# A fused transformer kernel with another written order of all its calls, and the cross attention's keys loaded from ScalarE's DMA queue

## The reference

```python
# block 0: 8 heads of 40, keys/values from the context, the last 4 context rows apart
hs      = mha(x @ Wq, enc @ Wk, enc @ Wv)                   # "FIRST"
ca_hs1  = mha(ca_q1, x, x)                                  # "CA": queries from the 4 rows
ca_hs2  = mha(ca_hs1 @ Wq, ca @ Wk_ca, ca @ Wv_ca)
x = (hs + ca_hs2) @ Wout + b_out + x
# block 1: 20 heads of 16
h1 = ln(x); x = attn(h1, h1, q1, k1, v1, o1) + x            # "SELF"
h2 = ln(x); x = attn(h2, context, q2, k2, v2, o2) + x       # "CROSS"
h3 = ln(x); a, g = split(h3 @ ff_w1 + ff_b1)
x = (a * gelu(g)) @ ff_w2 + ff_b2 + x                       # FF = 1280
```

## Time and profile before

| | |
|---|---|
| median of 3 runs | 3753.11 us (3748.72 to 3754.11) |
| the profiled execution, its time | 3752.51 us |
| its span, first to last instruction | 3750.7 us |
| mean granted TensorE clock | 0.959 |
| TensorE busy | 3433.0 us, 92% |
| VectorE, ScalarE, GpSimd busy | 61%, 65%, 56% |

### The profile page before, as it was taken

How to read it: one execution, slowest core, us unless ns; L and a number is a source line. 1 busy time by engine, 2 the same in 40 slices (tenths; PEclk the granted TensorE clock), 3 DMA queues, 4 the chain that set the end, 5 groups by cost and what they waited for, 6 DMA issues and landing times.

```text
span 3750.7 us, 114679 instructions
## 1 busy us (share of the span) xinstructions
PE 3433.0 (92%) x38842; PEld 2823.0 (75%) x38842; DVE 2282.8 (61%) x5540; ACT 2431.1 (65%) x4362; POOL 2082.5 (56%) x2307
## 2 busy tenths in 40 slices
PE   7799999999999999999999999999999999999998
PEld 6677777777777777777777777777777777777777
DVE  6566666566666656656665666666566666656664
ACT  3576666667766666776666677666666766666674
POOL 1556555555655555565555556555555655555564
PEclk6899999999999999999999999999999999999999
DMA  5211111221111122211112222111122211112220
GB/s 182 57 42 45 35 44 43 49 53 48 50 34 46 42 49 53 48 51 33 46 41 48 53 49 52 31 47 42 47 53 50 51 31 47 42 46 53 51 50 18
DMA packets 316267, 183.06 MB, mean 49 GB/s; under 512 B 50107, under 2 KB 315379, under 8 KB 315507
## 3 DMA queue, kind: packets, MB, share of 16 engines
q1 hardware_dynamic: 303936, 173.93, 18.4%
q10 hardware_dynamic: 11955, 3.04, 0.4%
HBM read 70.59 MB, written 24.67 MB: 25 GB/s over the span
## 4 chain that ended last, share of the span: by engine, by line
PE 35%; issue 29%; POOL 23%; DVE 8%; DMA 2%; POOLq 1%; ACT 1%; SPq 0%; DVEq 0%; ACTq 0%
PE bank L1487 32%; POOL PT L540 12%; POOL XB L517 2%; DVE mx L1104 2%; POOL cQ L547 2%; POOL cK L547 2%; DMA out<-X 2%; PE bank L1514 1%; POOL XA L517 1%; POOL rstd L598 1%; POOL c L592 1%; DVE OA L1219 1%; DVE hTn L1133 1%; POOL X L517 1%; DVE hTn L1130 1%
## 5 line engine op out<-in xcount | busy, mean ns | idle before, releaser
L540 POOL TENSOR_TENSOR PT<-P,PT 128x512 f16<-128x512 f32 (+1 forms) x924 | 1071.5, 1160 | 603.2 <-ACT PT L811 599.5
L1487 PE MATMUL bank<-hT,w_ff_w 128*128 128x256 f16 x5440 | 637.0, 272 | 0.8 <-DVE hT L1133 0.8
L1104 DVE TENSOR_REDUCE mx<-bank 128x4 f32<-128x512 f32 (+1 forms) x924 | 596.3, 683 | 56.1 <-PE bank L1487 49.4
L1487 PEld LDWEIGHTS bank<-hT,w_ff_w 128*128 128x128 f16 x5440 | 521.4, 98 | 60.7 <-DVE hT L1133 1.2
L1487 PE MATMUL bank<-mxs,pick 84*128 84x128 f16 (+1 forms) x3696 | 553.5, 230 | 0.0
L1487 PE MATMUL bank<-w_ff,F 128*128 128x320 f32 x1360 | 412.2, 438 | 41.6 <-DVE whole L1005 40.4
L1487 PE MATMUL bank<-Qs,Ks 96*128 96x128 f16 x2640 | 404.0, 235 | 15.1 <-DVE mxs L1113 15.1
L1487 PEld LDWEIGHTS bank<-mxs,pick 84*128 84x128 f16 (+1 forms) x3696 | 395.8, 109 | 4.1
L794 ACT ACTIVATE gate<-bank,ff_b,scale 128x256 f32<-128x256 f32 x340 | 187.5, 566 | 304.3 <-PE bank L1487 228.5
L1487 PEld LDWEIGHTS bank<-V,PT 128*128 128x128 f16 (+1 forms) x9504 | 317.0, 96 | 39.5 <-POOL PT L540 13.8
L1487 PE MATMUL bank<-V,PT 128*128 128x17 f16 (+1 forms) x9504 | 341.5, 173 | 0.0
(11 more groups left out here) (289 smaller groups left out, 7386.5 us busy)
## 6 DMA issues: line engine op xcount, KB each, us to landing
Qs<-cQ SPq DMA_DIRECT2D x402, 64.0 KB, 2.6
Ks<-scratch_k SPq DMA_DIRECT2D x99, 160.0 KB, 4.9
Ks<-cK SPq DMA_DIRECT2D x198, 64.0 KB, 2.6
Q0s<-cQ SPq DMA_DIRECT2D x198, 60.0 KB
K0s<-cK SPq DMA_DIRECT2D x198, 60.0 KB
xin<-in_x SPq DMA_DIRECT2D x34, 320.0 KB, 3.6
out<-X SPq DMA_DIRECT2D x64, 160.0 KB, 1.9
xT<-in_xT SPq DMA_DIRECT2D x68, 128.0 KB, 2.1
```

The lines of the kernel that those rows point to most:

```text
L540: nc.gpsimd.tensor_tensor(PT[0:keys, n % PT_SLOTS, 1, :], P[0:keys, n % P_SLOTS, :], PT[0:keys, n % PT_SLOTS, 0, :], ALU.subtract).then_in ...
L1104: nc.vector.tensor_reduce(mx[:, g % 2, 4 * u:4 * u + 4], bank[:, :].rearrange("p (h s) -> p h s", h=4)[:, :, 0:keys], axis=AX.X, op=ALU.ma ...
L1487: return nc.tensor.matmul(o, lhsT, rhs, start=start, stop=stop)
```

## The change

All calls of the loop are put into another order, on every engine, with `BODY` to match; the work of each call is the same. `ff0` is now the first job of a pass and `outM0_1` the last; `K0T1` goes between `outT1_1` and `outM1_0`, `K0T2` and `V0_1` into the cross attention's scores, `mT` and `mB` from behind `Q2T2` into the self attention; `S14` and `S15` stand within the down projection `y1`; `V1_0`, `V1_1` and `T2` go behind `S4`; gelu 2 and 3 go behind the exponentials of `T0` and `T1`. The three loads of the cross attention's keys are issued by ScalarE behind the exponentials of `T13`, no longer by SP.

```diff
 BODY = jobs_of("""
-    Q0T0 XT0_0 XT0_1 S0 Q0T1 Q0T2 K1T0 K1T1 K1T2 Q1T0 Q1T1 Q1T2 S1 ff0 S2 S3 ff1 ff2 mx0 K0T0 ff3 T0
-    V1_0 K0T1 mx1 K0T2 V0_0 T1 V1_1 T2 S4 S5 S6 S7 S8 T3 vca mx2 S9 T4 S10 T5 S11 T6 S12 S13 caT0
-    mx3 T7 T8 T9 T10 T11 T12 T13 caT1 ff4 outT1_0 ff5 ff6 ff7 outT1_1 outM1_0 outM1_1 ff8 XT1_0 ff9
-    XT1_1 s4 Q2T0 Q2T1 Q2T2 mT mB V0_1 K2T0 K2T1 y1 S14 S15 S16 S17 S18 mx4 S19 S20 T14 S21 T15 S22
-    S23 T16 S24 S25 mx5 T17 S26 T18 S27 mx6 T19 T20 T21 T22 p4T T23 T24 mx7 outT2_0 T25 y0 T26
-    outM2_0 V2_0 outT2_1 T27 hs0 outM2_1 outT0_0 hs1 XT2_0 V2_1 outT0_1 outM0_0 K2T2 outM0_1 XT2_1 G
+    ff0 Q0T0 Q0T1 XT0_0 Q0T2 XT0_1 ff1 K1T0 K1T1 S0 S1 K1T2 Q1T0 S2 S3 mx0 Q1T1 Q1T2 V0_0 mx1 T0 T1
+    ff2 ff3 S4 S5 T2 vca S6 S7 V1_0 T3 S8 S9 mx2 S10 K0T0 T4 S11 T5 S12 S13 T6 V1_1 mx3 T7 caT0 caT1
+    T8 mT T9 T10 T11 T12 T13 mB ff4 outT1_0 ff5 ff6 ff7 outT1_1 K0T1 outM1_0 outM1_1 ff8 s4 XT1_0
+    XT1_1 ff9 Q2T0 Q2T1 Q2T2 K0T2 S14 S15 y1 S16 S17 S18 V0_1 K2T0 mx4 S19 S20 S21 T14 S22 S23 K2T1
+    S24 T15 S25 mx5 T16 S26 T17 T18 T19 T20 p4T T21 mx6 S27 T22 T23 y0 mx7 T24 T25 K2T2 outT2_0 V2_0
+    outT2_1 T26 T27 outM2_0 hs0 outM2_1 outT0_0 hs1 V2_1 outM0_0 outT0_1 XT2_0 XT2_1 G outM0_1
 """)
...
             def one_pass(i, stores):
-                load_products(i)
                 put_low(i, "Q0T", 0, Q0s, cQ, Q_PARTS)
...
                 put_split(i, "Q1T", 2, Qs, cQ, Q_PARTS)
+                load_products(i)
                 load_next(i)
                 put_low(i, "K0T", 0, K0s, cK, K_PARTS)
                 put_low(i, "K0T", 1, K0s, cK, K_PARTS)
-                stack_cross_keys(i)
-                put_low(i, "K0T", 2, K0s, cK, K_PARTS)
                 put_split(i, "Q2T", 0, Qs, cQ, Q_PARTS)
                 put_split(i, "Q2T", 1, Qs, cQ, Q_PARTS)
                 put_split(i, "Q2T", 2, Qs, cQ, Q_PARTS)
-                put_out(i, 0, stores)
+                put_low(i, "K0T", 2, K0s, cK, K_PARTS)
...
+            def stack_cross_keys(i):
+                act.wait_ge(k2_put, i * CROSS_STORES + CROSS_STORES)
+                act.wait_ge(j_full, done(i, LOOP_JOBS.number("T13"), "J"))
+                for y, part in enumerate(K_PARTS):
+                    act.dma_start(Ks[y * D1:(y + 1) * D1, :, :],
+                                  s_k2[part, :, :].rearrange("(h e) n -> e h n", e=D1)).then_inc(cross_stacked, 16)
```

More of the change, by code:

```diff
@@ L882, in _ @@
                 links[0] = 0
+                gelu(i, L, 0)
                 high_chunk(i, "Q0T", 0, cQ, CH0[0], FQ0)
+                high_chunk(i, "Q0T", 1, cQ, CH0[1], FQ0)
                 high_blocks(i, "XT0_0", hTn, 0)
+                high_chunk(i, "Q0T", 2, cQ, CH0[2], FQ0)
                 high_blocks(i, "XT0_1", hTn, 1)
-                high_chunk(i, "Q0T", 1, cQ, CH0[1], FQ0)
                 split_context(i)
-                high_chunk(i, "Q0T", 2, cQ, CH0[2], FQ0)
+                gelu(i, L, 1)
                 high_shifted(i, "K1T", 0, cK, 0)
@@ L1397, in _ @@
                 normalise(i, 1)
+                extremes_x(i + 1)
+                extremes_context(i + 1)
+                low_part(i, "V1", 1, V1, HEADS1, D1, V1_FACTOR)
+                low_maxima(i, 3)
                 copy_hT(i, "caT0", 0, CH0)
-                low_maxima(i, 3)
+                copy_hT(i, "caT1", 1, CH0)
+                diagonal(i, L, 2)
                 normalise(i, 2)
-                copy_hT(i, "caT1", 1, CH0)
-                extremes_x(i + 1)
+                step_sizes(i, L)
                 ff(i, L, 4)
@@ L1409, in _ @@
                 low_out(i, 1, 1)
+                low_chunk(i, "K0T", 1, cK, CH0[1], FK0)
                 residual(i, 1, 0)
+                residual(i, 1, 1)
                 norm(i, 1, 0)
-                residual(i, 1, 1)
+                norm(i, 1, 1)
                 ff(i, L, 8)
-                norm(i, 1, 1)
+                scores4(i)
                 low_blocks(i, "XT1_0", hTn, 0)
+                low_blocks(i, "XT1_1", hTn, 1)
                 ff(i, L, 9)
-                low_blocks(i, "XT1_1", hTn, 1)
-                scores4(i)
                 whole_shifted(i, "Q2T", 0, 6)
@@ L1443, in _ @@
                 low_maxima(i, 5)
+                softmax4(i)
                 maxima(i, 26)
+                copy_shares(i)
+                low_maxima(i, 6)
                 maxima(i, 27)
-                low_maxima(i, 6)
-                copy_shares(i)
+                result(i, L, 0)
+                low_maxima(i, 7)
                 normalise(i, 4)
-                low_maxima(i, 7)
+                normalise(i, 5)
+                low_chunk(i, "K2T", 2, cK, CH1[2], FK2)
                 low_out(i, 2, 0)
-                result(i, L, 0)
-                normalise(i, 5)
-                residual(i, 2, 0)
                 low_part(i, "V2", 0, V2, HEADS1, D1, fixed[:, F2:F2 + 1])
@@ L1800, in _ @@
                 filled[0] = 0
+                ff(i, L, 0)
                 chunk(i, "Q0T", 0, "Wq", x16, PASSES_X, AT0, CH0)
+                chunk(i, "Q0T", 1, "Wq", x16, PASSES_X, AT0, CH0)
                 turn_norm(i, 0, 0)
+                chunk(i, "Q0T", 2, "Wq", x16, PASSES_X, AT0, CH0)
                 turn_norm(i, 0, 1)
-                scores(i, 0)
-                chunk(i, "Q0T", 1, "Wq", x16, PASSES_X, AT0, CH0)
-                chunk(i, "Q0T", 2, "Wq", x16, PASSES_X, AT0, CH0)
+                ff(i, L, 1)
@@ L1807, in _ @@
                 chunk16(i, "K1T", 0, "k1")
                 chunk16(i, "K1T", 1, "k1")
+                scores(i, 0)
+                scores(i, 1)
                 chunk16(i, "K1T", 2, "k1")
                 chunk16(i, "Q1T", 0, "q1")
+                scores(i, 2)
+                scores(i, 3)
+                turn_maxima(i, 0)
                 chunk16(i, "Q1T", 1, "q1")
                 chunk16(i, "Q1T", 2, "q1")
-                scores(i, 1)
-                ff(i, L, 0)
-                scores(i, 2)
@@ L1816, in _ @@
-                scores(i, 3)
-                ff(i, L, 1)
+                values(i, "V0", 0, "Wv")
+                turn_maxima(i, 1)
+                exponents(i, 0)
+                exponents(i, 1)
                 ff(i, L, 2)
-                turn_maxima(i, 0)
-                chunk(i, "K0T", 0, "Wk", c16, PASSES_C, AT0, CH0)
                 ff(i, L, 3)
-                exponents(i, 0)
-                values1(i, 0)
-                chunk(i, "K0T", 1, "Wk", c16, PASSES_C, AT0, CH0)
-                turn_maxima(i, 1)
@@ L1826, in _ @@
-                chunk(i, "K0T", 2, "Wk", c16, PASSES_C, AT0, CH0)
-                values(i, "V0", 0, "Wv")
-                exponents(i, 1)
-                values1(i, 1)
-                exponents(i, 2)
                 scores(i, 4)
                 scores(i, 5)
+                exponents(i, 2)
+                token_values(i)
                 scores(i, 6)
+                scores(i, 7)
+                values1(i, 0)
+                exponents(i, 3)
                 attend(i, 0)
-                scores(i, 7)
+                scores(i, 8)
@@ L1836, in _ @@
                 attend(i, 1)
-                scores(i, 8)
-                exponents(i, 3)
-                token_values(i)
+                scores(i, 9)
                 turn_maxima(i, 2)
-                scores(i, 9)
+                scores(i, 10)
+                chunk(i, "K0T", 0, "Wk", c16, PASSES_C, AT0, CH0)
                 exponents(i, 4)
-                scores(i, 10)
-                exponents(i, 5)
                 scores(i, 11)
                 attend(i, 2)
-                exponents(i, 6)
@@ L1876, in _ @@
                 turn_out(i, 1, 1)
+                chunk(i, "K0T", 1, "Wk", c16, PASSES_C, AT0, CH0)
                 out_proj(i, 1, 0)
@@ L1899, in _ @@
                 scores(i, 18)
+                values(i, "V0", 1, "Wv")
+                chunk(i, "K2T", 0, "k2", c16, PASSES_C, AT1, CH1)
                 turn_maxima(i, 4)
```

242 lines of the change are left out of this document (115 added, 127 removed).

## The result

Before 3751.79 us, after 3732.56 us (medians of 5 runs each, 3748.72 to 3754.11 and 3731.02 to 3738.58): ratio 0.9952, 95% interval 0.9938 to 0.9967. The change makes the kernel 0.5% faster, a quarter of the 2.0% that the forecast of 3680 us stood for. The profiled execution after took 3731.02 us.

What follows compares the result with a forecast made beforehand. TensorE was taken as the bound, busy 92%, with about 16 us of a 109.2 us pass lost. Terms of 57.65, 46.4 and 2.9 us made 107.0; over 33 passes -73 us, so 3680 us, range 3590 to 3755.

Steps and rivals of the forecast that it cites:

- So `S4` waits about 3.5 us: At S4, the first self-score tile: a new TensorE stall of about 3.5 us until Q1T's first chunk lands.
- about 2.9 us: Behind S4, from S4 to T4: the clock falls for 6.8 us and pushes the chain by about 2.9 us.
- 22.4 less 18.5: From the pass start: Q1T's first chunk lands at 22.4 us; TensorE's earlier work, with waits removed, ends at 18.5.
- base 7.58 for 7.15: S4 to T4's exponential without the clock's fall: forecast 7.15 us, from 6.03 plus 2.3 of work less 1.2 of waits.
- no fall of the clock: Rival at S4: a shorter stall or surrounding work keeps the clock up; 104.1 us a pass, 3585 us, chance 0.20.
- The low clock 3.3: Between Q2T0 and the next pass: the half-speed stretch behind mx4 goes away, saving 3.3 us a pass.
- "0.5 us" for the key loads: At ScalarE behind T13's exponential: three key-load issues cost 0.5 us, within bounds of 0 and 3.1.
- if ScalarE stands for its own loads: Sign of failure at the three key loads; the forecast expected ScalarE idle under 1 us there.
- The slower rival, late inputs: Next inputs late at extremes_x, delaying T9 and bringing a second TensorE stall; about 3860 us, chance 0.17.
- VectorE idle before `extremes_x` about 4 us: Sign in the new trace: VectorE, there at 30.8 us, idles about 4 us for inputs landing at 34.5.
- The forecast's price for two late things, added up: Late S4 plus inputs 3 us late: T9 2.5 to 3.5 us late, 2.9 more for the clock; at 5.4, 112.4 a pass.

Runs made afterwards that it cites:

- b_fill: Kernel before the change with 24 extra matmuls of 256 columns put into mx4's bank before its wait for the maxima: 3720.88 us, ratio 0.9913.
- a_fill: Changed kernel with 36 extra matmuls of 256 columns put into S4's bank before its wait and overwritten by S4: 3657.74 us, ratio to before 0.975.
- a_pairs: Changed kernel with SyncE's copies of K1T and Q1T issued in pairs, in the order S4 to S8 need them: 3730.18 us.
- b_keys: Kernel before the change with only the cross attention's three key loads moved to ScalarE, between T13's exponentials and gelu 4: 3789.3 us, ratio 1.0099.

## Why the prediction was only half right

Direction and mechanism held in the main: a new stall at `S4` with only the landing of `Qs` as releaser; the low clock behind `S4` and none behind `mx4`; `mx4` waiting 0.3 us, `y1` not at all; six table loads a pass (4428 activations for 4362); SyncE's first copy at 4.8 us (forecast 4.9); `Q2T0` to the next pass 46.3 us (46.4), `T4`'s exponential to `Q2T0` 27.9 (28.1). What failed is the size of two terms ahead of `T4`; two more terms of the sum deserve a look.

**The size of "So `S4` waits about 3.5 us" and of the "about 2.9 us" for the clock.** This is the step that failed. The forecast's pass is 107.0, the measured one 108.78. Of the difference 1.1 us are at `S4` (23.47 for 22.4), 1.1 behind it (11.13 for 10.05); the other stretches are 0.3 better. Against a forecast gain of 2.2 us a pass that is nearly everything.

The first: by its own terms, 22.4 less 18.5, the forecast should have said 3.9 us; the wait measured 4.4. From the first copy to the third issue of `Q1T0` it took 15.8 us for 14.96, because one copy of `K1T2` (the first of its three in 18 of 30 passes, the second in 11) takes about 1.6 us instead of 0.6; the last 0.2 us lie behind the landing. The forecast took the lengths of before, where such an issue mostly came in `Q1T`, behind the place that counts.

The second: base 7.58 for 7.15, and 3.55 for 2.9. The price of the fall was right: passes in which the clock is low for 6.83 us, the length that it had in all passes before, take 10.56 us from `S4` to the exponential, 3.0 more than the base. But in 20 of 30 passes it is low for 10.24 us, and those take 11.41, 3.8 more. The trace shows what goes with the length: where it is 10.24 us, the fall came 1.4 to 2.4 us ahead of `S4`, still in the wait; where it is 6.83, between 1.2 us ahead of `S4` and 0.5 behind it.

The case "no fall of the clock" was given 0.20 and 3585 us; with the fall behind `S4` taken away and nothing else it was 3658, since inputs came late.

**"The low clock 3.3" that was booked as a gain behind `mx4`.** `b_fill` puts it at 1.0 as long as `mx4`'s wait stands, with 1.2 more that VectorE's maxima take up. The stretch still came out at 46.3, so other terms of the same sum were wrong by about 2 us the other way; which ones, no run shows. A right sum here isn't proof of its parts.

**"0.5 us" for the key loads.** In the kernel after it came out so, 0.53 us (27.86 for 27.33); in the kernel before the same loads cost 1.0. The reason given for the value, an empty queue, was not the point: one issue is often long on ScalarE too, and even with three short ones ScalarE stood for 0.53 us. The sign "if ScalarE stands for its own loads" did show, on average under the 1 us that was allowed for.

The slower rival, late inputs, hardly came about in the kernel after. Eight of 33 passes have a wait at `mT`, 5.0 us in all. The trace shows why: in the pass shown `extremes_x` starts at 2100.22, with no wait, 38.3 us into the pass, since the stall and the low clock in front had made VectorE later than the load that was issued at 2095.81. So the sign "VectorE idle before `extremes_x` about 4 us" failed (0.14 us on average). The forecast had VectorE there at 30.8, which is 8.4 us behind its `S4`; even with the clock up, in `a_fill`, it is there 11.1 us behind `S4`. Late inputs were the next limit, hidden under the first: TensorE waits 1.3 us a pass for them in `a_fill`, 2.5 in `a_pairs`. The forecast's price for two late things, added up, doesn't hold when one covers the other.

Where the expected gain went: the order itself gave 5.7 us a pass from `Q2T0` on and 0.4 ahead of `S4`; `S4`'s stretch took 5.1 back (11.13 for 6.03), of which 3.55 are clock, and the one to `Q2T0` another 0.5 (27.86 for 27.37), which is what the loads on ScalarE cost there. About the rule of the Trainium skill in "DMA: Bandwidth & Descriptors", "Issuing engines are not separate DMA queues", by which the other issuing engine saves only issue time: the runs agree for SyncE, where nothing was gained (in `b_keys` no stretch is shorter than before), and show what it leaves out here, that the issuing engine pays.

Left open: why the fall of the clock comes at different places around the same wait, and why single issues take about 1 us more.

## What to carry to other kernels

Price a stall on TensorE with the clock behind it, but by the stretch: 6.83 us at the lower clock cost 3.0 us where TensorE's chain was the bound, and 1.0 where VectorE's maxima were close behind; a few throwaway matmuls in the wait measure it, and are a remedy. When a serial DMA queue feeds a row of tiles, issue in the order in which the tiles need the chunks, and then look at once for the next thing in that queue: here the pairs gave nothing until the read of the next inputs was moved about 3 us back, and the two together gave 3.5%. Leave issues off the engine that is the bound at that place.

## What was not expected of the hardware

- An edit that adds 36 matmuls a pass makes the kernel 75 us faster (3733 to 3658).
- 6.83 us at a granted clock of 0.50 cost 0.96 us in one place and 3.0 in another; 10.24 us of it 3.8 there.
- Behind the wait at `S4` the low stretch was 10.24 us long in the 20 passes in which the clock fell at least 1.4 us before TensorE's work began again, and 6.83 us in the 10 in which it fell later.
- The length of one DMA issue: 0.32 to 0.85 us usually, and 1.2 to 2.0 us in about one pass of two or more, on SyncE and on ScalarE, mostly at one place in a kernel and at another in the next.
- ScalarE's queue issues DMAs while its activations are in the pipe (2038.03 to 2039.37, above), so that three issues can cost it nothing.
